# A Perceiver layer with top-2 experts: the table of expert slots written by indirect stores instead of one-hot products

## The reference

```python
# xn: the 4096 normalised tokens, [4096, 256]
p = sigmoid(logits * routing_bias)                  # [4096, 7]
top2 = the two largest of each row, ties to the lower number
w    = p[top2] / sum(p[top2])
y    = silu(xn @ shared_gate) * (xn @ shared_up) @ shared_down
y   += sum over c in 0, 1 of  w[c] * expert(top2[c], xn)
out  = x2 + y
# expert(e, t) = (silu(t @ gate[e]) * (t @ up[e])) @ down[e], hidden width 704
```

## Time and profile before

| | |
|---|---|
| three timed runs | 1595.52, 1596.11, 1599.26 us; median 1596.11 us |
| the profiled execution | 1593.83 us, of which the span from first to last instruction is 1592.0 us |
| mean granted TensorE clock | 0.96 of full speed |
| busy, share of the span | PE 90%, DVE 68%, ACT 53%, POOL 48% |
| chain that ended last | PE 56%, DVE 24%, ACT 11%, issue 4%, DMA 3% |
| attention part | from 0 to about 930 us |
| shared tiles 0 to 9 | from 934 to about 1077 us |
| routed tiles 10 to 44 | from about 1080 to 1475 us, PE busy almost without a break |

### The profile page before, as it was taken

One profiled execution on the slowest core, in us unless ns is written; L12 is line 12 of the kernel. 1 busy time (PEld: TensorE's weight loads), 2 busy tenths in 40 slices (PEclk: granted clock), 3 DMA queues, 4 the chain that ended last, 5 costly groups with the idle time before them and its releaser, 6 DMA issues.

```text
span 1592.0 us, 43384 instructions
## 1 busy us (share of the span) xinstructions
PE 1434.0 (90%) x17186; PEld 1074.6 (68%) x17186; DVE 1085.5 (68%) x1972; ACT 847.2 (53%) x1838; POOL 761.4 (48%) x677
## 2 busy tenths in 40 slices
PE   3788998999999999999999665999999999999987
PEld 1456675666666666666666454887888888887865
DVE  2886889888888888888888459784444444443357
ACT  1566876777778777777687422452323232322221
POOL 1575677777677767676766310002333333332110
PEclk9899999999999999999999678999999999999998
DMA  4586776777677777767685343552422222221182
GB/s 136 115 167 125 148 136 124 141 132 144 137 139 142 137 149 135 150 129 146 119 155 97 74 101 70 139 156 70 74 67 74 68 74 68 74 68 55 38 267 74
DMA packets 464497, 183.62 MB, mean 115 GB/s; under 512 B 414608, under 2 KB 452832, under 8 KB 464304
## 3 DMA queue, kind: packets, MB, share of 16 engines
q1 hardware_dynamic: 454128, 149.25, 47.3%
q0 software_dynamic: 10176, 31.60, 5.7%
HBM read 61.77 MB, written 17.56 MB: 50 GB/s over the span
## 4 chain that ended last, share of the span: by engine, by line
PE 56%; DVE 24%; ACT 11%; issue 4%; DMA 3%; SPq 1%; POOL 1%; DVEq 0%; POOLq 0%
PE ps L1022 22%; PE ps L1050 10%; PE ps L748 9%; DVE experts L1392 6%; ACT experts L1128 4%; PE ps L740 4%; DVE work L1523 4%; ACT experts L1115 3%; PE ps L765 2%; DVE experts L1480 2%; PE ps L735 2%; PE ps L792 2%; DVE experts L1431 1%; DMA work<-token_in 1%; PE ps L1055 1%
## 5 line engine op out<-in xcount | busy, mean ns | idle before, releaser
L1022 PE MATMUL ps<-work,experts 128*128 128x256 f16 (+1 forms) x3630 | 403.7, 272 | 42.1 <-DMA work<-token_in 13.4
L1022 PEld LDWEIGHTS ps<-work,experts 128*128 (+1 forms) x3630 | 340.0, 100 | 97.6 <-issue 15.6
L748 PE MATMUL ps<-experts 128*128 128x512 f16 (+2 forms) x2304 | 363.8, 309 | 31.4 <-DVE work L1536 14.7
L748 PEld LDWEIGHTS ps<-experts 128*128 128x128 f16 x2304 | 198.2, 100 | 174.5 <-DVE work L1536 28.9
L1115 ACT ACTIVATE work<-work 128x768 f16<-128x768 f32 (+1 forms) x134 | 99.3, 741 | 368.5 <-PE ps L1055 234.4
L1128 ACT ACTIVATE experts<-ps,experts 128x256 f32<-128x256 f32 x512 | 203.8, 474 | 74.9 <-DVE experts L1392 74.8
L627 POOL TENSOR_TENSOR experts<-experts 128x1024 f16<-128x1024 f32 x96 | 191.7, 1996 | 61.0 <-ACT experts L1115 61.0
L694 POOL DMA_INDIRECT work<-token_in,work x70 | 68.0, 972 | 309.2 <-DMA work<-work 216.1
L1050 PE MATMUL ps<-experts,work 128*128 (+1 forms) x1530 | 187.8, 276 | 3.7 <-DVE work L1700 3.7
L1050 PEld LDWEIGHTS ps<-experts,work 128*128 128x128 f16 x1530 | 146.9, 99 | 28.7 <-DVE work L1700 4.0
L1392 DVE TENSOR_REDUCE experts<-ps 128x4 f32<-128x1024 f32 x128 | 155.9, 1219 | 12.7 <-PE ps L765 11.7
(11 more groups left out here) (211 smaller groups left out, 2184.4 us busy)
## 6 DMA issues: line engine op xcount, KB each, us to landing
experts<-in_ctx SPq DMA_DIRECT2D x32, 512.0 KB, 5.0
experts<-choice_out POOLq DMA_DIRECT2D x8, 1024.0 KB, 13.1
experts<-in_x SPq DMA_DIRECT2D x32, 128.0 KB, 2.3
token_in<-experts SPq DMA_DIRECT2D x32, 128.0 KB, 2.9
work<-in_L_ffn_routed_gate SPq DMA_DIRECT2D x8, 352.0 KB, 3.1
experts<-experts SPq DMA_TRANSPOSE x160, 4.6
work<-in_L_ffn_routed_up SPq DMA_DIRECT2D x8, 320.0 KB, 4.4
out<-x_all POOLq DMA_DIRECT2D x5, 512.0 KB, 3.3
```

Of the source, the lines that this page charges most:

```text
L748: ins = pe.matmul(bank, lhs[a][k], rhs[b][k], start=(k == 0 and a + b == 0), stop=(last and k == len(lhs[0]) - 1 and a == 1))
L1022: ins = pe.matmul(out[:, r * n:(r + 1) * n], experts_h[:, e, lo:lo + P], e_rows_t[k][:, b * DK + kk, r * n:(r + 1) * n], start=(kk == 0 an ...
```

## The change

The product of one-hot matrices goes; POOL writes the table itself.

A DRAM table `slot_rows` [128 * 70] of int32 is filled with spare row numbers by one transfer of POOL during the attention part. In tile 1 DVE works out `slot_at` = lane * 70 + half for each choice (one more instruction on 64 values). When that is there, POOL issues 64 indirect stores, each of which writes 128 row numbers of 4 bytes to the places that one column of `slot_at` names. It waits for all of them to land and loads the table back as `row_out` (128 x 70). DVE takes `row_in` from it with one instruction, `read_slots`, which now waits for that load and stands ahead of `hidden(8, 0)` (`TABLE` goes from 4 to 8).

The routing on DVE is cut in four: `route_starts` ahead of `hidden(1, 0)`, `route_places` behind `hidden_low(1, 0)`, `route_slots` behind `hidden_low(1, 1)`, `route_experts` behind `hidden_low(2, 1)`. PE's 64 matmuls and its waits around them go; it waits for the last routing step ahead of tile 10. The chunks per tile go from (0, 2, 2, 3, 3, 3, 3, 4, 4, 4) to (0, 0, 2, 3, 3, 4, 4, 4, 4, 4). SP's loads of chunks 22 and 23 wait for the last routing step and no more for the table.

```diff
-                  ("one", 1), ("tile", NEXP), ("desc", NE), ("iota", P), ("rowid", TOPK), ("spare", 2),
-                  ("tnum", NTILE)):
+                  ("one", 1), ("tile", NEXP), ("desc", NE), ("rows", TOPK * NTILE), ("spare", 2 * NSLOT)):
...
+    slot_rows = nc.dram_tensor("slot_rows", [P * 2 * NSLOT, 1], I32, kind="Internal").ap()
...
             if CHUNK_PLACE[n] >= 5:
-                sp.wait_ge(S["table_ready"], 1)
+                sp.wait_ge(S["route_step"], ROUTE_DONE)
...
+            if s == 4:
+                pool.dma_start(slot_rows.rearrange("(p j) o -> p (j o)", p=P), const("spare").bitcast(I32))\
+                    .then_inc(S["spare_written"], 16)
+
+        def write_rows(c):
+            pool.wait_ge(S["route_step"], ROUTE_PARTS)
+            for t in range(NTILE):
+                k = c * NTILE + t
+                pool.indirect_dma_start(
+                    out=slot_rows, out_offset=bass.IndirectOffsetOnAxis(ap=slot_at.bitcast(U32)[:, k:k + 1], axis=0),
+                    in_=const("rows").bitcast(I32)[:, k:k + 1], in_offset=None).then_inc(S["rows_written"], 16)
...
+        pool.wait_ge(S["spare_written"], 16)
+        for c in range(TOPK):
+            write_rows(c)
+        pool.wait_ge(S["rows_written"], 16 * TOPK * NTILE)
+        pool.dma_start(row_out.bitcast(I32), slot_rows.rearrange("(p j) o -> p (j o)", p=P)).then_inc(S["slots_read"], 16)
         pool.wait_ge(S["table_ready"], 1)
         for t in range(FIRST, MID):
             gather(t)
...
-        for t in range(1, TABLE):
+        for t in range(1, FIRST):
             tile(t, t % 2, SHARED, SHARED)
-
-
-        pe.wait_ge(S["lane_hot_ready"], TOPK)
-        pe.wait_ge(S["route_step"], ROUTE_HOT)
-        pe.wait_ge(S["y_ready"], TABLE - 1)
-        for c in range(TOPK):
-            for t in range(NTILE):
-                ins = pe.matmul(ps[:, 7, 0:4 * NSLOT], lane_hot[:, c, t, :],
-                                half_hot[:, c, t, :, :].rearrange("p v j -> p (v j)"),
-                                start=(c == 0 and t == 0), stop=(c == TOPK - 1 and t == NTILE - 1))
-        ins.then_inc(S["slot_mm"], 1)
-        pe.wait_ge(S["slots_read"], 1)
-
-        for t in range(TABLE, FIRST):
-            tile(t, t % 2, SHARED, SHARED)
+        pe.wait_ge(S["route_step"], ROUTE_DONE)
         pe.wait_ge(S["chunk_lo_ready"], NCHUNK * NE)
...
-            if n == 2 * NCHUNK:
-                act.wait_ge(S["slot_mm"], 1)
...
-            link(v.tensor_copy(r_half, r_half_i))
+            v.tensor_copy(r_lane, r_lane_i)
+            link(v.tensor_copy(r_half, r_half_i))
+            link(v.scalar_tensor_tensor(out=slot_at.rearrange("p (c t) -> p c t", c=TOPK), in0=r_lane, scalar=2.0 * NSLOT, in1=r_half,
+                                        op0=ALU.mult, op1=ALU.add))
...
         def read_slots():
 
-            dve.wait_ge(S["slot_mm"], 1)
...
+            dve.wait_ge(S["slots_read"], 16)
+            v.tensor_scalar(row_in.bitcast(I32), row_out.bitcast(I32), NB * SQ - 1, None, ALU.bitwise_and)\
+                .then_inc(S["table_ready"], 1)
...
-        for t in range(1, TABLE):
+        for t in range(1, FIRST):
+            if t == 1:
+                route_starts()
+            if t == TABLE:
+                read_slots()
             hidden(t, 0)
             chunks(t, 0)
             shared_result(t - 1, t - 1)
             hidden_low(t, 0)
-            if t <= TOPK:
-                lanes_of(t - 1)
-                half_of(t - 1)
+            if t == 1:
+                route_places()
             chunks(t, 1)
             hidden(t, 1)
             hidden_low(t, 1)
-            if t <= TOPK:
-                half_rows(t - 1)
-                half_tiles(t - 1)
+            if t == 1:
+                route_slots()
+            if t == 2:
+                route_experts()
...
-TABLE = 4
-CHUNKS_AT = (0, 2, 2, 3, 3, 3, 3, 4, 4, 4)
+TABLE = 8
+CHUNKS_AT = (0, 0, 2, 3, 3, 4, 4, 4, 4, 4)
```

More of the change, by code:

```diff
@@ L104, in constants @@
     put("desc", np.arange(NE, 0, -1)[None, :])
-    put("iota", np.arange(P)[None, :])
-    put("rowid", p[:, None] * NTILE + NB * SQ * np.arange(TOPK)[None, :])
-    put("spare", TOPK * NB * SQ + 1 + p[:, None] + P * np.arange(2)[None, :])
-    put("tnum", 1 + np.arange(NTILE)[None, :])
+    rows = p[:, None, None] * NTILE + NB * SQ * np.arange(TOPK)[None, :, None] + np.arange(NTILE)[None, None, :]
+    put("rows", rows.reshape(P, -1).astype(np.int32).view(np.float32))
+    spare = TOPK * NB * SQ + p[:, None] + P * (np.arange(2 * NSLOT) % 2)[None, :]
+    put("spare", spare.astype(np.int32).view(np.float32))
     ck, sk = rope(np.arange(SK), 1.0 / W_SCALE)
@@ L298, in program @@
     row_out, row_in = (place2(2 * NSLOT) for _ in range(2))
+    slot_at = place2(TOPK * NTILE).bitcast(I32)
     tile_e = place2(FIRST + NEXP).bitcast(I32)
@@ L339, in program @@
     r_lane_i, r_half_i = (ct(place3(TOPK * NTILE).bitcast(I32)) for _ in range(2))
-    r_found = place3(2 * 2 * NSLOT).rearrange("p (v j) -> p v j", v=2)
-    r_none, r_row = (place3(2 * NSLOT) for _ in range(2))
     ps = stack.enter_context(nc.psum_tensor("ps", [P, 8, 512], F32))
@@ L1773, in _ @@
-        for c in range(TOPK):
-            link(v.tensor_tensor(r_c, r_oh[c], r_pos, ALU.mult))
-            link(v.tensor_reduce(r_slot[:, c, :], r_c, AX.X, ALU.add))
-        link(v.tensor_copy(r_lane_i, r_slot))
-        link(v.tensor_scalar(r_half_i, r_lane_i, P.bit_length() - 1, None, ALU.arith_shift_right))
-        link(v.tensor_scalar(r_lane_i, r_lane_i, P - 1, None, ALU.bitwise_and))
-        link(v.tensor_copy(r_lane, r_lane_i))
-        link(v.tensor_copy(r_half, r_half_i))
-        assert count[0] == ROUTE_PARTS
@@ new lines, in route_places, with route_slots @@
+        def route_places():
+            link(v.tensor_tensor(r_pos, r_cum, r_tot, ALU.subtract))
+            link(v.tensor_tensor(r_pos, r_pos, r_in, ALU.add))
+            link(v.tensor_tensor(r_eq, r_pos, bc(r_limit, 1, NTILE), ALU.is_ge))
+            v.tensor_tensor(r_pos, r_pos, bc(r_start, 1, NTILE), ALU.add)
+            link(v.tensor_tensor(r_eq, r_eq, bc(r_jump, 1, NTILE), ALU.mult))
+            link(v.tensor_tensor(r_pos, r_pos, r_eq, ALU.add))
+        def route_slots():
+            for c in range(TOPK):
+                link(v.tensor_tensor(r_c, r_oh[c], r_pos, ALU.mult))
+                link(v.tensor_reduce(r_slot[:, c, :], r_c, AX.X, ALU.add))
+            link(v.tensor_copy(r_lane_i, r_slot))
+            link(v.tensor_scalar(r_half_i, r_lane_i, P.bit_length() - 1, None, ALU.arith_shift_right))
+            link(v.tensor_scalar(r_lane_i, r_lane_i, P - 1, None, ALU.bitwise_and))
+            v.tensor_copy(r_lane, r_lane_i)
+            link(v.tensor_copy(r_half, r_half_i))
+            link(v.scalar_tensor_tensor(out=slot_at.rearrange("p (c t) -> p c t", c=TOPK), in0=r_lane, scalar=2.0 * NSLOT, in1=r_half,
+                                        op0=ALU.mult, op1=ALU.add))
+            assert count[0] == ROUTE_PARTS
@@ new lines, in route_experts @@
+        def route_experts():
+            odd_halves = slice(NFULL, NEXP)
+            link(v.tensor_tensor(r_t, bc(const("tile"), 2, NE), bc(r_even_to, 1, NEXP), ALU.is_ge))
+            link(v.tensor_reduce(r_tf, r_t, AX.X, ALU.add))
+            link(v.tensor_tensor(r_t[:, 0:2 * NMIX, :], bc(const("tile")[:, odd_halves], 2, NE), bc(r_odd_end, 1, 2 * NMIX), ALU.is_ge))
+            v.tensor_scalar(r_tm, r_tf[:, odd_halves], float(NE), None, ALU.is_ge)
+            link(v.tensor_reduce(r_to, r_t[:, 0:2 * NMIX, :], AX.X, ALU.add))
+            link(v.scalar_tensor_tensor(out=r_to, in0=r_to, scalar=-float(NE), in1=r_tm, op0=ALU.add, op1=ALU.mult))
+            link(v.tensor_tensor(r_tf[:, odd_halves], r_tf[:, odd_halves], r_to, ALU.add))
+            link(v.tensor_scalar(r_tf, r_tf, 1.0, float(NE), ALU.add, ALU.min))
+            link(v.memset(tile_e, 0))
+            link(v.tensor_copy(tile_e[:, FIRST:FIRST + NEXP], r_tf))
@@ L1884, in _ @@
             hidden_low(t, 1)
-            if t <= TOPK:
-                half_rows(t - 1)
-                half_tiles(t - 1)
-        assert count[0] == ROUTE_HOT
-        read_slots()
-        for t in range(TABLE, FIRST):
-            shared_tile(t)
+            if t == 1:
+                route_slots()
+            if t == 2:
+                route_experts()
+        assert count[0] == ROUTE_DONE
         hidden(FIRST, 0)
@@ L1954 @@
 ROUTE_PARTS = ROUTE_SELECTED + 4 + 2 + NE + 9 + 5 + 2 * TOPK + 5
-ROUTE_HOT = ROUTE_PARTS + 9 + 3 * TOPK
+ROUTE_DONE = ROUTE_PARTS + 9
 _SPARE = NCHUNK * (NE - 2)
```

81 lines of the change are left out of this document (19 added, 62 removed).

## The result

The change makes the kernel slower: 1647.85 us, median of four runs (1645.70 to 1650.35), against 1596.28 us for the kernel before beside it. The ratio is 1.032, with a 95% interval of 1.029 to 1.035. The forecast was 1591.2 us with a range up to 1604, so it was wrong by 57 us and on the wrong side.

The account below looks back on a forecast made before the run. PE bounds the routed tiles, which move as a block, so only tile 10's start counts: 26.4 us gained less a stall of 21.5 is 4.9 us, giving 1591.2 us against a median of 1596.11; range 1570 to 1604.

Parts of the forecast that it names:

- What PE gains if the table costs nothing: Ahead of tile 10: fewer PE pauses, no table matmuls, higher clock; tile 10 begins at 1053.3, a gain of 26.4 us.
- The distance of two stores: POOL's row of 64 stores: 1.31 us from one to the next, taken from pairs of scatters; ends 0.72 and 2.4 us.
- DVE holds POOL up: Rival, row of stores: POOL stands still during `chunk_low`, table at 1078.9, kernel ends 20 us later, 1616; chance 0.05.
- 0.03 us per store: Row of stores: what a DVE instruction with two SBUF operands adds to each POOL store, counted inside the 1.31 us.
- The wait that this adds: Tile 8: DVE, PE and ACT stop for the table until 1053.7; tile 10 follows 21.1 us later, at 1074.8; stall 21.5 us.
- the rival that loses from 1.39 us on: POOL's stores in tiles 2 to 8 are slower: 1.51 us apart gives 1603.8 us, 2.4 us gives 1660; chance 0.22.
- that PE, DVE and ACT work on undisturbed beside POOL's row of stores: Tiles 2 to 8: the row costs other engines nothing until the wait in tile 8; tiles follow every 11.36 us.
- no pause over 1 us on PE from 947 to 1037: Sign expected in the profile after: PE runs without long pauses until its stop in tile 8, from about 1037.
- slower stores by the pace of the transfer engines: Rival, tiles 2 to 8: 8192 writes of 4 bytes make the row run at the transfer engines' pace; chance 0.22.

Follow-up runs that it names:

- e1: Changed kernel without its 64 indirect stores, the table a fixed one that the fill writes: 1565.58 us.
- e14: Changed kernel with one single wait for the landing, after the eighth store: 1599.73 us.
- e18: Changed kernel, its 64 stores in one row, with `route_experts` behind tile 3's work in place of tile 2's: 1593.25 us.
- e4: Changed kernel with 64 stores of 1 KB rows into a table nobody reads, and a fixed slot table: 1600.76 us.
- e5: Changed kernel, its 64 stores of 4-byte rows going to an array that nothing else fills or reads, with a fixed table: 1652.99 us.
- e11: Changed kernel with a POOL memset of 128 x 128 elements behind each store: 1647.48 us.
- e16: Changed kernel with stores of 64 rows in place of 128, 4 bytes a row, into an array nobody reads, with a fixed table: 1600.09 us.
- e13: Changed kernel with rows of 768 bytes into an array nobody reads, and a fixed table: 1597.12 us.
- e3: Changed kernel with a wait for the landing after every four stores: 1625.71 us.
- e12: Changed kernel with waits after every 8 stores and DVE's read of the table at tile 9 instead of tile 8: 1604.90 us.
- e15: Changed kernel, its stores beginning only behind DVE's last routing step: 1607.79 us.
- e17: Changed kernel with one wait after the eighth store and DVE's table read behind tile 9 instead of ahead of tile 8: 1591.34 us, median of six.
- e8: Changed kernel with waits for the landing after every 16 stores: 1644.50 us.
- e6: Changed kernel with 64 more transposes at PE's very start, moving PE's later code by 128 instructions: 1652.54 us.
- e2: Kernel before, keeping its one-hot table, with 64 stores of 4-byte rows added in POOL's idle time into a table nobody reads: 1595.52 us.

## Why the prediction was wrong, step by step

**What PE gains if the table costs nothing: right.** Without stores tile 10 begins at 1053.53 us (forecast 1053.3), and e1 takes 1565.58 us. Against the trace of the kernel before its span is 28.2 us shorter, of which 26.2 us lie ahead of tile 10 (forecast 26.4). The 34.1 us to the single execution beside it, 1599.65, hold in addition what single executions differ by.

**The distance of two stores: right for the bare instruction, wrong for the place.** Forecast 1.31 us by the pairs of scatters. Beside idle engines it is 1.265 us, for rows of 4 to 1024 bytes alike. Beside a working DVE it is more. In e14 the first store is at 969.42 and the last at 1060.14, 1.44 us on the mean, 1.1 us in all for the one wait included; e18 has no wait and 1.44 us too. The forecast's rival "DVE holds POOL up" had the right cause: its 0.03 us per store was taken from a scatter beside one subtraction of 1.03 us, and `chunk_low`, which reads two operands in SBUF for 0.95 to 1.6 us, makes a store of 0.96 us one of up to 2.0 us. So of this sum the term "0.03 us per store" was mis-sized; it is 0.17 (1.44 less 1.265). That the changed kernel itself comes out at the forecast's 1.31 us on the mean is luck: DVE stood still beside most of its stores.

**The wait that this adds: right.** Once the crawl is away, DVE waits in `read_slots`, PE stops in tile 8, and from DVE's read to tile 10 it is 21.6 us (1064.66 to 1086.26 in e14; forecast 21.1). From the first store to tile 10 it is 116.8 us, against 108.9 in the forecast. The 7.9 us between are the distance, by which the sum would be 63 x (1.44 - 1.31) = 8.2 us. The forecast gained 4.9 us by its sum; less 7.9 that is 3.0 us lost. From PE's first expert matmul to tile 10 it is 149.7 us in e14 and 148.4 in e18, against 145.7 in the kernel before: 4.0 and 2.7 us lost. (By the times e14 lost 3.9 us and e18 gained 4.6, within what single executions differ by.) Even without the crawl, then, the change as written was about even with the kernel before or a little behind it, on the side of the rival that loses from 1.39 us on.

**The step that failed: that PE, DVE and ACT work on undisturbed beside POOL's row of stores.** The forecast put the cost of the row for the other engines at nothing: tiles follow each other every 11.36 us up to tile 8, with "no pause over 1 us on PE from 947 to 1037", and the row's only price is a late table. What the traces show in its place is the crawl, from 981 to 1062 us, some 48 us long in its effect: the changed kernel takes 165.6 us from the first store to tile 10, e14 116.8. No rival of the forecast held this. The one on the losing side, slower stores by the pace of the transfer engines, ended above 1600 too, but its mechanism is refuted: the stores in the changed kernel were 1.31 us apart on the mean (63 from 970.12 to 1052.48), as forecast, the engines were nearly idle, and e4 with 256 times the bytes was 47 us faster. I had looked for what DVE's work would do to POOL, and not for what POOL's row would do to the others.

**What of the crawl is shown.** The state comes with stores of 128 rows with up to 512 bytes each, in a row of more than eight without a wait, with DVE's ten small instructions beside the sixth to eighth: eight kernels have all of this (the changed one and e5 to e11), and all eight crawl, from 11.0 to 11.6 us behind the first store. With any one of them taken away it didn't come, in one execution each: the number of rows (e16), their bytes (e4, e13), the row without a wait (e3, e14; moments of it in e12), its place (e15), or the small instructions from their place (e18, where the work of DVE behind them comes sooner too). Only for the wait after the eighth store are there more executions, the six of e17, none of which took longer than 1599.00 us. And e12 beside e14 shows that these conditions don't settle all of it. Once there the crawl lasts until 3 to 10 us behind the last store, through pauses of 1.1 us (e8). It is not a shortage of transfer engines (share 0.07) or of anything in the array written to (e5), and neither e6 nor the packets of instructions speak for a shortage of fetched code. What in the chip couples POOL's stores to the issue of PE and the starts of ACT and DVE stays open; so does whether and why those small instructions set it off, since e2 had the same ones beside its first two stores and ran on.

## What to carry to other kernels

Many small indirect transfers in one row are cheap by their own count and can still cost the whole core. Test them in their real place with a single wait put in, or with a neighbour moved by a tile; if the time falls by many times the length of the wait, it was never the transfers' own price. Do it in more than one execution each.

Cost a POOL transfer by the distance of two (1.265 us here, whatever the bytes), and add what DVE's instructions with two operands in SBUF beside it take away: 0.17 us per store on the mean here.

Where a late result is needed by one tile only, put the engine's wait for it behind all work that doesn't need it: that alone gave 8.1 us here.

## What was unexpected in the hardware

- PE issued one instruction in 1.40 us, and ACT and DVE stood for 67 and 59 us with what they waited for done some 60 us before, while POOL issued stores every 1.265 us; the transfer share was 0.07.
- A one-line wait of 1.1 us after the eighth store was worth 48 us (e14).
- An indirect store takes POOL 0.96 us and 0.30 us to the next, for rows of 4, 64, 512, 768 and 1024 bytes; with 64 rows in place of 128 it is 1.20 us from one to the next.
- A DVE product of 4.42 us with two operands in SBUF made a store of 0.96 us last 4.03 us.
